# Softplus by one ScalarE table, ternary weights by Sign, and a reordered Mamba layer in a two-layer gated block

## What is computed

```python
# first stage, per batch
u = silu(conv(in_proj_w @ ctx) + conv_b)
x_dbl = x_proj_w @ u                       # 16 rows of dt, 16 of B, 16 of C
delta = softplus(dt_proj_w @ dt_lo + dt_proj_b)
A = -exp(A_log)
state = state * exp(d_t * A) + (d_t * u_t) * B_t      # scan over 512 positions
y_t = sum_n(state * C_t);  y = (y + D * u) * silu(z)
# second stage: every weight matrix becomes ternary
gamma_w = clip(mean(abs(w)), 1e-5)
w_dq = clip(round(w / gamma_w), -1, 1) * gamma_w
# x = x + tanh(g_xattn[0]) * mamba(ctx, layernorm(x))
# x = x + tanh(g_ffn[0])   * bit_ffn(layernorm(x))
# x = x + tanh(g_xattn[1]) * cross_attention(layernorm(x), ctx)
# x = x + tanh(g_ffn[1])   * experts(layernorm(x))
```

## Time and profile before

| what | value |
|---|---|
| median of 3 runs | 1902.91 us (1902.73 to 1903.48) |
| span of the profiled execution (the page gives no other time for it) | 1906.4 us |
| TensorE (PE) | 1763.0 us busy, 92% |
| VectorE (DVE) | 1358.1 us, 71% |
| ScalarE (ACT) | 981.7 us, 51% |
| GpSimd (POOL) | 655.3 us, 34% |
| DMA | 300.31 MB, mean 158 GB/s |
| chain that ended last | PE 64%, DVE 14%, issue 7%, ACT 6%, DMA 4%, POOL 4% |

### The profile page before, as it was taken

One profiled execution on the slowest core, in us unless ns is written; L12 is line 12 of the kernel. 1 busy time (PEld: TensorE's weight loads), 2 busy tenths in 40 slices (PEclk: granted clock), 3 DMA queues, 4 the chain that ended last, 5 costly groups with the idle time before them and its releaser, 6 DMA issues.

```text
span 1906.4 us, 19429 instructions
## 1 busy us (share of the span) xinstructions
PE 1763.0 (92%) x6054; PEld 803.1 (42%) x6054; DVE 1358.1 (71%) x1963; ACT 981.7 (51%) x1926; POOL 655.3 (34%) x677
## 2 busy tenths in 40 slices
PE   8853999978999999999999999999998989999999
PEld 3321343434444344444443444444444334444543
DVE  2778888899988889989988999897752444431321
ACT  6889665545575455575646465565334333330100
POOL 1222351135565224554632164473202433320100
PEclk9976999989999999999999999999998999999999
DMA  7798992377884115797612368872111699855210
GB/s 256 218 257 232 268 281 71 106 208 186 189 217 121 35 34 127 163 256 198 185 37 54 92 156 234 203 177 78 34 56 45 191 282 268 241 166 214 83 50 34
DMA packets 163175, 300.31 MB, mean 158 GB/s; under 512 B 18937, under 2 KB 51705, under 8 KB 160129
## 3 DMA queue, kind: packets, MB, share of 16 engines
q1 hardware_dynamic: 145792, 236.14, 39.4%
q0 software_dynamic: 17280, 62.92, 16.9%
HBM read 177.64 MB, written 58.33 MB: 124 GB/s over the span
## 4 chain that ended last, share of the span: by engine, by line
PE 64%; DVE 14%; issue 7%; ACT 6%; DMA 4%; POOL 4%; SPq 0%; DVEq 0%; POOLq 0%; ACTq 0%
PE p L781 8%; PE p L792 8%; PE p L758 7%; PE p L741 7%; PE p L828 6%; PE p L634 5%; PE p L720 4%; PE p L715 4%; DVE s_M L957 3%; PE p L843 3%; PE p L764 3%; PE p L681 2%; DVE s_M L952 2%; DVE s_M L962 1%; POOL s_U L1478 1%
## 5 line engine op out<-in xcount | busy, mean ns | idle before, releaser
L957 DVE TENSOR_TENSOR_SCAN s_M<-s_M 128x1024 f32<-128x1024 f32 x128 | 296.7, 2318 | 13.0 <-ACT s_M L1209 10.5
L1100 DVE CUSTOM_DVE_ANT_0 s_U<-p,s_U 128x512 f32<-128x512 f32 x256 | 187.0, 745 | 147.4 <-PE p L758 145.9
L758 PE MATMUL p<-s_U 128*128 128x512 f32 x512 | 268.0, 612 | 4.6 <-DVE s_U L1100 3.4
L1433 POOL DMA_DIRECT2D s_u<-s_M x120 | 112.1, 934 | 463.5 <-DVE s_M L962 418.1
L741 PE MATMUL p<-s_U 128*128 128x512 f32 x512 | 251.8, 600 | 8.3 <-DMA s_U<-in_Wq 3.3
L1478 POOL TENSOR_SCALAR s_U<-s_U 128x512 f32<-128x512 f32 x256 | 242.2, 966 | 6.6
L792 PE MATMUL p<-s_U 128*128 128x512 f32 x512 | 224.3, 593 | 0.0
L781 PE MATMUL p<-s_U 128*128 128x512 f32 x472 | 213.7, 593 | 2.6 <-ACT s_U L1342 2.6
L1209 ACT ACTIVATE s_M<-s_dl,s_small 128x511 f32<-128x511 f32 x256 | 170.4, 716 | 37.2 <-DVE s_M L957 37.1
L1342 ACT COPY s_U<-p 128x512 f32<-128x512 f32 x196 | 105.0, 592 | 162.2 <-PE p L764 160.7
L1337 ACT ACTIVATE s_U<-s_U 128x512 f32<-128x512 f32 x256 | 181.6, 710 | 5.5 <-ACT s_U L1333 0.4
(11 more groups left out here) (178 smaller groups left out, 2424.6 us busy)
## 6 DMA issues: line engine op xcount, KB each, us to landing
s_u<-s_M POOLq DMA_DIRECT2D x120, 512.0 KB, 7.6
s_bc<-bc_scratch SPq DMA_DIRECT2D x128, 256.0 KB, 4.6
k_scratch<-s_U SPq DMA_DIRECT2D x16, 1024.0 KB, 7.0
v_scratch<-s_U SPq DMA_DIRECT2D x16, 1024.0 KB, 4.9
s_U<-in_Wq SPq DMA_DIRECT2D x64, 256.0 KB, 6.9
s_U<-k_scratch SPq DMA_DIRECT2D x64, 256.0 KB, 6.4
s_U<-rk_scratch SPq DMA_DIRECT2D x64, 256.0 KB, 7.0
s_U<-in_Wo SPq DMA_DIRECT2D x64, 256.0 KB, 4.2
```

The lines of the kernel that those rows point to most:

```text
L758: e.matmul(banks[bk][:], qT[j % 3][:, k * 128:(k + 1) * 128], kT[j % 2], start=True, stop=True).then_inc(S["a_s"], 1)
L957: e.tensor_tensor_scan(w, dA[i % 2], w, 0.0, ALU.mult, ALU.add).then_inc(S["m_s"], 1)
L1100: e.tensor_tensor_reduce(out=Pm[j % 2][:, k, :], in0=banks[ABANK[kind, j, k]][:], in1=rkb[j % 2], scale=rq[:, k:k + 1], scalar=-3.0e38, op ...
```

## The change

Softplus becomes one ScalarE function, over two halves; Abs, Relu, Exp, Ln and six VectorE passes go, as does the + 1. The clip goes: ScalarE's Sign, with a column of -MAGIC as its bias, turns the rounded number into -1, 0 or 1 as it writes eight bits. D * u moves from VectorE to POOL. For batch 0, Silu and x_proj go tile by tile, and the decay of two terms is made ahead instead of one. The small constants are prepared in other places. In the planner, a chunk of the second and third matrix is costed at 9.0 for its transfer instead of 5.0, K comes ahead of Q on ScalarE up to K's step 120 instead of 60, and the costs of M's steps are new.

```diff
@@ QUANT and MAMBA @@
     for c in range(5):
         QUANT += [("rnd", w, c)] if c < 4 else []
         QUANT += [("put", w, c - 1)] if c else []
-        QUANT += [("clip", w, c)] if c < 4 else []
...
+def mamba_order(b):
+
+    ahead = 1 if b else 2
+    order = [(k, t) for t in range(4) for k in ("in", "conv")]
+    order += [(k, t) for t in range(4) for k in ("silu", "xp")] if b == 0 else [("silu", 4), ("xp", 4)]
+    order += [("dt", t) for t in range(4)] + [("sp", 0), ("soft", 0), ("soft", 1), ("init", 0), ("dv", 0)] + [("decay", i) for i in range(ahead)]
+    last = 2 * NS - 2
+    for i in range(last):
+        order += [("mul", i), ("scan", i), ("decay", i + ahead), ("out", i)] + ([("ln", i - last + 4)] if i >= last - 4 else [])
...
+MAMBA = [mamba_order(b) for b in range(NB)]
@@ weights() and plan() @@
-            out.append(("Q", [("DMA", 5.0 if w else (17.0, 4.0, 9.0, 5.0)[c]), ("ACT", 2.0)], [(0, "put", w - 1, c)] if w else [], (0, kind, w, c), [], []))
+            out.append(("Q", [("DMA", 9.0 if w else (17.0, 4.0, 9.0, 5.0)[c]), ("ACT", 2.0)], [(0, "put", w - 1, c)] if w else [], (0, kind, w, c), [], []))
...
-            key = max(ready, free[e]), FIRST[e].index("N" if s == "M" and name[0] else "L" if s == "K" and e == "ACT" and i < 60 else s)
+            key = max(ready, free[e]), FIRST[e].index("N" if s == "M" and name[0] else "L" if s == "K" and e == "ACT" and i < 120 else s)
@@ vector @@
-                    elif kind == "clip":
-                        e.wait_ge(S["q_rnd"], 4 * w + c + 1)
-                        e.tensor_scalar(stg[c], stg[c], MAGIC - 1.0, MAGIC + 1.0, ALU.max, ALU.min).then_inc(S["q_cut"], 1)
...
                     elif kind == "soft":
...
+                        ts = slice(2 * i, 2 * i + 2)
+                        if b == 0 and i == 0:
+                            scaled_bias()
+                        e.wait_ge(S["m_sp"], 2 * b + i + 1)
+                        e.tensor_tensor(du[:, ts, :], dl[:, ts, :], u[:, ts, :], ALU.mult).then_inc(S["m_dl"], 1)
                     elif kind == "init":
-                        e.wait_ge(S["m_dl"], b + 1)
-                        for t in range(4):
-                            e.tensor_scalar(u[:, t, :], u[:, t, :], Dv[:, t:t + 1], None, ALU.mult).then_inc(*v.up())
@@ scalar @@
-                        e.wait_ge(S["q_cut"], i + 1)
-                        e.activation(dst, stg[c], ACT.Copy, bias=-MAGIC, saturate=False).then_inc(S["q_put"], 1)
+                        e.wait_ge(S["q_rnd"], i + 1)
+                        if i == 0:
+                            e.wait_ge(S["p_set"], 9)
+                        e.activation(dst, stg[c], ACT.Sign, bias=magic[:, 0:1], saturate=False).then_inc(S["q_put"], 1)
...
-                        e.activation(M0[:, i, :], banks[bk][:], ACT.Abs, bias=dtb[:, i:i + 1]).then_inc(*v.up())
-                        e.activation(du[:, i, :], banks[bk][:], ACT.Relu, bias=dtb[:, i:i + 1]).then_inc(S["m_re"], 1)
...
+                        e.activation(M0[:, i, :], banks[LBANK[b, "dt", i]][:], ACT.Identity, bias=dtb[:, i:i + 1]).then_inc(S["m_re"], 1)
+                    elif kind == "sp":
+                        e.wait_ge(S["m_re"], 4 * b + 4)
+                        for g in range(2):
+                            e.activation(dl[:, 2 * g:2 * g + 2, :], M0[:, 2 * g:2 * g + 2, :], ACT.Softplus).then_inc(S["m_sp"], 1)
@@ gpsimd @@
+                    if kind == "dv":
+                        for t in range(4):
+                            e.wait_ge(S["m_dl"], 2 * b + t // 2 + 1)
+                            e.tensor_scalar(u[:, t, :], u[:, t, :], Dv[:, t:t + 1], 1.0, ALU.mult, ALU.mult).then_inc(S["m_dv"], 1)
...
+                        if i < 2:
+                            e.wait_ge(S["m_dv"], 4 * b + 2 * i + 2)
```

More of the change, by code:

```diff
@@ L63 @@
         QUANT += [("put", w, c - 1)] if c else []
[L64 removed]
     if w == 1:
         QUANT += [("bias", 0, k) for k in range(3)]
[L68 to L75 removed]
+def mamba_order(b):
[6 more added lines that the diff above has]
+        order += [("mul", i), ("scan", i), ("decay", i + ahead), ("out", i)] + ([("ln", i - last + 4)] if i >= last - 4 else [])
+    order += [("mul", last), ("scan", last)] + [("decay", last + 1)] * (2 - ahead) + [("out", last), ("hn", 0), ("hn", 1), ("add", last)]
+    order += [("mul", last + 1), ("scan", last + 1), ("gate", 0), ("hn", 2), ("hn", 3), ("out", last + 1), ("add", last + 1), ("gate", 1)]
+    return order + [("yt", t) for t in range(4)]
+MAMBA = [mamba_order(b) for b in range(NB)]
 def ffn_order():
@@ L208, in mamba, with part @@
     out = []
-    def part(name, does, *needs):
-        bank = [LBANK[x] for x in [(b, *name)] if x in LBANK]
-        out.append(("M", does, [(b, *n) if isinstance(n[0], str) else n for n in needs], (b, *name), bank, bank))
-    for kind, i in MAMBA:
+    def part(name, does, *needs, take=(), free=()):
+        out.append(("M", does, [(b, *n) if isinstance(n[0], str) else n for n in needs], (b, *name), [LBANK[(b, *x)] for x in take], [LBANK[(b, *x)] for x in free]))
+    for kind, i in MAMBA[b]:
+        own = [(kind, i)]
@@ L223, in mamba @@
         elif kind == "soft":
-            part((kind, i), [("DVE", 1.3)], ("one", 0), *([(0, "put", 2, 3)] if b == 1 else []))
+            part((kind, i), [("DVE", 1.25)], ("sp", 0), *([(0, "put", 2, 3)] if b == 1 else []))
         elif kind == "init":
-            part((kind, i), [("DVE", 2.3), ("ACT", 1.4)], ("soft", 7))
+            part((kind, i), [("DVE", 0.2)], ("soft", 1))
+        elif kind == "dv":
+            part((kind, i), [("POOL", 4.3)], ("soft", 1))
+        elif kind == "decay":
+            part((kind, i), [("ACT", 1.43)], ("scan", i - (1 if b else 2)) if i >= (1 if b else 2) else ("init", 0))
@@ L227, in mamba @@
         elif kind == "mul":
-            part((kind, i), [("DVE", 1.35)], *([("out", i - NW)] if i >= NW else []))
+            part((kind, i), [("DVE", 1.25)], *([("out", i - NW)] if i >= NW else []))
         elif kind == "scan":
-            part((kind, i), [("DVE", 2.45)] + ([("ACT", 1.4)] if i + 1 < 2 * NS else []), ("scan", i - 1) if i else ("init", 0))
+            part((kind, i), [("DVE", 2.35)], ("decay", i))
         elif kind == "out":
-            part((kind, i), [("DVE", 1.3)] + ([("POOL", 0.8), ("SUM", 5.0)] if i < 2 * NS - 2 else []))
+            part((kind, i), [("DVE", 1.27)] + ([("POOL", 0.8), ("SUM", 5.0)] if i < 2 * NS - 2 else []))
@@ L241, in mamba @@
         elif kind == "yt":
-            part((kind, i), [("PE", 0.5), ("DVE", 0.8)], ("gate", 1))
+            part((kind, i), [("PE", 0.5), ("DVE", 0.8)], ("gate", 1), take=own, free=own)
     return out
@@ L298, in weights @@
             out.append(("Q", [("ACT", 2.0)], [(0, "thr", w, 0)], (0, kind, w, c), [], []))
-        elif kind == "clip":
-            out.append(("Q", [("DVE", 1.3)], [(0, "rnd", w, c)], (0, kind, w, c), [], []))
         elif kind == "put":
-            out.append(("Q", [("ACT", 2.0)], [(0, "clip", w, c)], (0, kind, w, c), [], []))
+            out.append(("Q", [("ACT", 2.0)], [(0, "rnd", w, c)], (0, kind, w, c), [], []))
         else:
@@ L1217, in act_mamba @@
                     elif kind == "silu":
-                        for t in range(4):
+                        for t in range(4) if i == 4 else [i]:
                             e.wait_ge(S["m_ac"], 4 * b + t + 1)
                             e.activation(u[:, t, :], ac[:, t, :], ACT.Silu).then_inc(S["m_u"], 1)
-                    elif kind == "xp":
+                        if b == 0 and i == 3:
+                            gates()
+                    elif kind == "xp" and i >= 3:
                         e.wait_ge(S["m_xp"], b + 1)
```

133 lines of the change are left out of this document (56 added, 77 removed).

## The result

The changed kernel takes **1873.41 us** (median of 4 runs, 1870.66 to 1878.58) against 1903.2 us of the kernel before beside it (4 runs, 1902.73 to 1904.61): ratio 0.9847, 95% interval 0.9829 to 0.9864, so 29 us faster. The forecast was 1875 us, and faster by over 0.2% was its likeliest case. How the 29 us come about was forecast less well, as will be seen. The profiled execution took 1878.6 us, the slowest of the four and 5 us above their median; its span is 1876.7 us.

The account below looks back on a forecast made before the run. PE, busy for 92% of the span, was taken as the bound, with its idle time to win. 18 us up to attention's start plus 10 us behind it, 28 us, off the median before gave 1875 us; range 1842 to 1905 us.

Parts of the forecast that it names:

- The first scan: Start of the first batch: its first scan starts at about 43 us instead of 70.4, 27 us earlier.
- T: End of the product with C of the first batch's 31st term: 229 us by full transfers, 265.0 before.
- long waits of DVE for B and C: Sign of being wrong: DVE waiting long for transfers of B, C or the terms.
- The rivals of more, no and less DMA limit: Transfers up to T: DMA gives more, 1856 us (0.15); sets no limit, 1836 us (0.03); gives less, 1894 us (0.15).
- the slower case: Rival: DMA reaches only 0.81, T is 271 us, attention starts 24 us late, 1917 us in all (chance 0.10).
- From T to attention: Attention starts at T + 181.4 us, so at 410 us instead of 428.0: 18 us won.
- The 13 us from T to the mean: Wait at the third mean for its last chunk: 1.5 us of issues, 9 to land, 2.1 for magnitudes and sum.
- 5 us of PE waiting at the mean: Sign of being right: the third mean's wait is 5 us or more on PE.
- Behind 428 us: After attention's start: 10 us won over two periods, middle of nothing and 20.5 us; nothing counted in the third.
- PE above 96% in both periods: Sign of being right: PE busy for more than 96% of the two attention periods.
- The rival of no relief: Behind attention's start PE is the only bound, so only 18 us are won: 1885 us (chance 0.13).
- The rival that the change does not reach the path: Whole kernel: Softplus halves cost 2 us, loads grow, gains are waited for elsewhere: 1903 us (chance 0.04).

Follow-up runs that it names:

- late_scan: The changed kernel with twenty more VectorE passes, 24.4 us, in front of the first batch's first scan: 1899.38 us, ratio 0.9974.
- plan_undone: The changed kernel with the planner's two numbers put back (5.0 for a chunk, keys first on ScalarE for 60 steps): 1924.26 us, ratio 1.0116.
- dma_more: The changed kernel with four unused copies of 1 MB more on SP's queue in the first batch: 1889.75 us, ratio 0.9929.
- chunk7: The changed kernel with 7.0 instead of 9.0 us for a chunk in the planner: 1864.14 us, ratio 0.9793.
- dve_more_later: The changed kernel with eight more VectorE passes in a block ahead of the scans of each of batches 1 to 3: 1909.45 us, ratio 1.0032.
- plan_alone: The kernel before with only the planner's two numbers changed (9.0 for a chunk, 120 steps): 1909.05 us, ratio 1.0029.
- dve_more_spread: The changed kernel with eight more VectorE passes in each of batches 1 to 3, one in front of every fourth scan: 1909.01 us, ratio 1.0023.
- dve_less: The changed kernel with a VectorE product left out for 8 of 32 terms in each of batches 1 to 3: 1877.88 us, ratio 0.9861.
- clip_back: The changed kernel with VectorE's clip put back between rounding and Sign, in kernel and planner: 1869.08 us, ratio 0.9814.

## Why the prediction was right, and where it was not

**The first scan**: 43 us forecast, 45.1 measured (the terms that I listed add up to 41.7). **New passes**: Softplus's half at 1.048 us is the bound that I took (1.05), Sign is 2.005 us (2.01), the table loads are 1283 ns each still, and D * u is hidden on POOL (1.04 us a tile in the mean; POOL waits for DVE, and nobody waits for it). That the earlier scan counts in full is not shown: late_scan cost 24 us for 24.4, but with everything else held up too, and in plan_undone the first scan is at 44.3 us and attention still starts at 438.7.

**T**: 229 forecast, 226.5 measured. The step by which it was taken, transfers at a share near 1 and not VectorE's chain, is borne out by three things: the share of 1.01 from 45 us to T, 22.8 us of VectorE's waits for B and C, and 15 us of bytes in dma_more, which moved T by 10.2 us and the time by 16. T alone would not tell, since VectorE's chain allowed 223 us. I had listed long waits of DVE for B and C as a sign of being wrong; they are what full transfers look like from VectorE. The rivals of more, no and less DMA limit fell with it, and the slower case, which decides from T = 257 us, was far off.

**From T to attention**: attention starts at 412.7 us, 410 forecast: 15.3 us won, not 18. PE's 168.4 us of work behind the mean came out as 168.5. The 13 us from T to the mean were 17.7: SP issued the last chunk at 231.9 us, 5.4 us behind T and not 1.5, the magnitudes' sum was there 9.6 us after that, and PE, still at a block of values, came to the mean 2.7 us later. This was the mis-sized term. chunk7, whose list has that load ahead, had the mean 6.4 us earlier and attention's start with it; the other 4 us of its 10 came behind attention's start or are noise. The sign I gave for it, 5 us of PE waiting at the mean, was wrong: PE waited 6.3 and 6.5 us for key copies and then found the mean ready.

**Behind 428 us**: 10 us forecast, 14.4 measured (29.7 of the spans less 15.3). The number came near by luck, for the place was wrong. I had put the relief into the first two periods, half of 20.5 us, and nothing into the third. From PE's first matmul to the end of the first two periods the kernel takes 1.0 us more than before, and the third period alone is 15.8 us shorter. So two steps failed. The first is "I take 10 us for both, the middle": the bound of nothing was right, and PE's idle time from its first matmul of attention to the third mark went from 28.9 to 30.9 us, in spite of some 10 us less on VectorE in each. The second is "In the third period DVE already waits, ... so I count nothing there". Busy time in before (first row) and after (second), from the third mark to the fourth:

```profile
1125.80:1466.90 341.10, 325.92 (x1260) 155.09 (x1252) 258.45 (x392) 176.60 (x386) 135.76 (x149) 0.98 0.47 123
```

```profile
1111.50:1436.80 325.30, 319.50 (x1260) 152.52 (x1252) 239.33 (x380) 171.08 (x378) 128.28 (x144) 1.00 0.44 117
```

PE runs the same 1260 matmuls in both. Its idle time goes from 15.2 to 5.8 us, which is 9.4 of the 15.8 us; the other 6.4 are its busy time, at a granted clock of 0.98 before and 1.00 after. In before, the end of the last batch's ternary FFN and its turning fall into this period: PE waits 1.7 us for ACT ahead of 1434 us (L681) and 4.7 us for DVE ahead of 1443 us (L693), and from 1440 us the clock is near its lower level (1.2 GHz):

```profile
1440.00:1451.00 11.00, 7.49 (x21) 4.99 (x22) 4.01 (x10) 2.34 (x4) 3.38 (x8) 0.53 0.00 0
```

(In the expectation of dve_more_later this period is said to end at 1429 us in the change; its mark is at 1436.8. The idle time given there is right.)

VectorE has 19 us less to do in the period, though no Softplus falls there: the last batch's scans start 60.0 us ahead of the third mark before and 89.8 us ahead in after, so 21 of them are left and not 25. In before and plan_alone, with a lead of 60 us, the period takes 341 and 340 us; with leads of 89.8 to 93.2 us it takes 325 to 327 us in ten of eleven kernels. The eleventh is dve_more_spread, which puts 6.7 us of VectorE into it: 334 us. dve_less takes 5.9 us of VectorE out of it and stays at 326 us. So the period answers to VectorE's load down to about the load of the change, and not below. But plan_undone, with a lead of 160 us and 12 scans left, takes 336 us, so the lead is not all, and no run changed the lead alone: as a cause it is argued and not shown. The sign "PE above 96% in both periods" held for one only: 94.5% and 97.3% of 428 to 775 and 775 to 1120 us.

**The rival of no relief** (1885 us) fell by its number, but for the first two periods its reason, that PE is the only bound there, fits the trace and dve_less better than my sum; what it missed is the third period. **The rival that the change does not reach the path** fell too, but was nearer than I thought: plan_undone is 22 us slower than the kernel before. I had treated the planner's numbers as a detail of the first batch. They are what turns the rest into a gain, and the parts do not add up: plan alone +6, all but the plan +22, together -29 us.

What stays open: why the order of the change needs 353.8 us from PE's first matmul of attention to the second mark, where before needs 349.6, chunk7 349.1 and clip_back 344.1 (PE is idle for 21.7 us in the change, 16.9 in before and 14.5 in clip_back; two of its waits, 4.3 and 3.5 us at 434 and 451 us, are for DVE's softmax pass), and how much of the 29 us is relief: parts that do not add up forbid such a split.

## What to carry over

Where a planner or a hand-written order fixes the lists, judge an edit together with its costs in the planner: the same 29 us more of VectorE cost 18 us when planned and 35 when not, and about as much taken away without telling the planner won nothing. Compare stages by the same mark in both kernels, and split what a stage gained into idle time and clock: counted from DVE's first softmax pass and not from PE's first matmul, 6.9 us of this change's gain would stand in periods that gave none. Ask of every list which single load or matmul at its end gates the next stage, and where it stands: one number in the planner that put a 1 MB load ahead of its neighbour won a third as much as the whole change. When one stage has the transfers full, count bytes; engine passes removed there are worth little.
